# The first job's row maxima computed at the end of the token stage in front of each attention, in a two-layer decoder on one core

## The chip, the core and the metric

The program runs on one core of a Trainium2 chip. The metric is the device time of one execution in microseconds (us). The engines are TensorE (PE in the profile, its weight loads PEld), VectorE (DVE), ScalarE (ACT), GpSimd (POOL) and SyncE (SP), which here issues nearly all DMAs. All of them run their own instruction streams in order and meet at semaphores.

## The reference

Two decoder layers over x of 2 x 1024 tokens with 256 features (16 heads of 16), each layer post-normalised:

```
x = layernorm(x + L0_attn(x))          # ALiBi, heads 0-7 look back, heads 8-15 look forward
x = layernorm(x + L0_xattn(x, ctx))    # 154 context tokens, scores clipped at +-10000
x = layernorm(x + L0_ffn(x))           # 8 experts, top 2
x = layernorm(x + L1_attn(x))          # full attention
x = layernorm(x + L1_xattn(x, ctx))    # 154 context tokens
x = layernorm(x + L1_ffn(x))           # a causal attention (MLA), then 8 experts, top 2

attn = softmax(q @ k.T / 4)            # over the keys, for each head
out  = attn @ v
```

A softmax needs the maximum of each row of scores before the exponential.

## The kernel before

The program is a list of stages: t0, at0, t1, xa0, t2, routing, experts, t3, at1, t4, xa1, t5, mla, t6, routing, experts, t7. Between two stages every engine drains and adds to one semaphore, and waits for all five: a barrier. at0, at1 and mla are self-attentions, xa0 and xa1 cross-attentions, the t stages ("token stages") do projections, layer norms and the q, k, v matmuls. The five places at which a token stage is followed by an attention are t0/at0, t1/xa0, t3/at1, t4/xa1 and t5/mla.

**An attention stage.** The 16 heads are four sets of 4 heads and the batch has two entries, which makes 8 groups `(s, i)`: `s`, the slot, is 0 or 1 (first or second half of each tensor of queries and keys, 64 of 128 output rows; in at0 slot 0 looks back and slot 1 forward), `i` the rest. A group has two jobs, one for each half of the 1024 queries. A job first computes its row maxima: TensorE makes the scores of 128 queries against all keys that count ("A" events, `pe_max`, L1535 and the diagonal mask L1538; L1789 in the cross-attention) into one of two PSUM regions of two banks each (banks 0 to 3), and VectorE reduces them to one column (`dve_max`, L1651; L1637 where it also adds the mask; L1890 in the cross-attention). In the causal and ALiBi stages the first job has 6 such units and the second 16; in at1 every job has 16 of 1024 keys; in the cross-attentions every job has 4. Then the maxima are transposed ("MT", L1585, L1835), negated (L1658, L1898), split into three bf16 parts by four instructions on GpSimd (`pool_split`), and `load_max` (L1460, L1736) copies these by three DMAs on SP's queue into three extra rows of the queries. Only then can the job's scores with the maximum subtracted be made ("ST", `pe_scores`, L1559; L1807), exponentiated (L1618, L1874) and multiplied with v ("PV", L1577), copied out ("OC", L1678) and transposed and divided ("OT", L1592, L1691).

`plan()` simulates an attention stage with fixed costs and writes the order of all these events into `at.events`; TensorE and VectorE follow that list in order. `LEAD` is 8 us.

**The queue of SP in an attention stage** before: rows of ones for three groups, `load_group` of group 1 (three loads of queries, six of keys, in at0 two of ALiBi rows), `load_max` of job 0, in at0 `rows_and_weights` (weights of t1 and the whole x), then jobs and groups in turn. In the cross-attentions it is the queries of group 1 (three DMAs), then `load_max` of job 0.

**A token stage** has for each half of a batch entry (512 tokens, halves 0 to 3) one "unit" for each of two f (f = 0 and 1 are the two blocks of 128 outputs) of q and k, and two for v: two to eight matmuls each (L1074, L1077, L1088, L1082), in order half 0, half 1, half 2, half 3. A q or k unit is split into three bf16 parts (L981/L984 on ScalarE, L1188/L1185 on VectorE, L990 on ScalarE, L893 on GpSimd) and stored to DRAM by two DMAs (`store_unit`, L831; `q_halves`, `k_parts`). `make_plan()` lists all this as tasks with a cost and a lag, and `list_order` schedules them greedily by the length of the path behind each, tries 150 shifted ranks, and keeps the order with the earliest end. Tasks of one kind stay in order. Each engine follows its own list in order. The task `ahead` waits on SP until the stores of halves 0 and 1 have landed and loads group 0 of the attention (`load_first`; L679 and L683, or L667). t0 also holds the context's keys and values (`ContextPart`; its matmuls use banks 0 to 3), and at its end SP stores the values, two DMAs of 1 MB (`store_values`, L1300); the first OT of at0 waits for them on VectorE (`rows_free`).

`mstat2`, the tile of maxima, is cleared by VectorE as the first instruction of each attention stage (L1696, L1924), so that row shows when the stage begins.

## Time and profile before

| | us |
|---|---|
| runs shown (3) | 2197.24, 2198.05, 2199.29; median 2198.05 |
| the profiled execution's own time | 2198.73 |
| its span, first to last instruction | 2197.0 |
| PE busy | 1950.5 (89%) |
| DVE busy | 1282.9 (58%) |
| ACT busy | 1015.5 (46%) |
| POOL busy | 482.0 (22%) |

A busy share is a mean over 17 stages. The granted clock of TensorE has two levels, 1.2 and 2.4 GHz; a row of a window gives the mean of the two as a share of the full one (0.50 is 1.2 GHz throughout). Beside each instruction the timeline gives the idle time of the engine ahead of it and who ended it.

### The profile page before, as it was taken

How to read it: one execution, taken by the hardware profiler on the slowest of the kernel's cores; microseconds unless marked ns; L12 is line 12 of the kernel's file. 1: busy time of each engine (PE TensorE's matmuls, PEld its weight loads, DVE VectorE, ACT ScalarE, POOL GpSimd, SP SyncE). 2: the span in 40 equal slices, each digit the busy share in tenths (PEclk: the TensorE clock that was granted, in tenths of full speed). 3: DMA queues.
4: the chain of work that ended last, by engine and by line, in shares of the span. 5: the costliest groups of instructions: out<-in, count | busy, mean ns of one | idle time of the engine just before them, and what ended most of it. 6: DMA issues, size and time to landing. Idle time of an engine off the chain costs nothing. (4 is left out here: it accounts for less than half of the span.)

```text
span 2197.0 us, 32881 instructions
## 1 busy us (share of the span) xinstructions
PE 1950.5 (89%) x10990; PEld 1009.5 (46%) x10991; DVE 1282.9 (58%) x2302; ACT 1015.5 (46%) x1953; POOL 482.0 (22%) x825
## 2 busy tenths in 40 slices
PE   8799999787689999968999999987887999977993
PEld 4344445332656666633223222253453444464662
DVE  3578774686622222246888888646586787653114
ACT  3156665576211111133566666754542666632333
POOL 2221101323132222212100000022352101033441
PEclk9599999898689999988899999998997999977997
DMA  7643222420811000037221111034234333051224
GB/s 195 166 64 53 43 33 52 109 46 16 354 44 33 31 31 31 29 114 156 30 30 30 30 30 30 1 97 101 45 78 107 53 59 60 2 192 41 64 63 134
DMA packets 98871, 157.90 MB, mean 72 GB/s; under 512 B 31415, under 2 KB 78839, under 8 KB 93559
## 3 DMA queue, kind: packets, MB, share of 16 engines
q1 hardware_dynamic: 86898, 131.55, 26.0%
q0 software_dynamic: 7488, 20.46, 3.0%
q10 hardware_dynamic: 4352, 4.20, 0.6%
q8 instruction: 74, 1.21, 0.3%
q14 instruction: 59, 0.48, 0.1%
HBM read 110.44 MB, written 44.72 MB: 71 GB/s over the span
## 5 line engine op out<-in xcount | busy, mean ns | idle before, releaser
L1618 ACT ACTIVATE arena<-psum 128x512 f32<-128x512 f32 (+1 forms) x1120 | 574.8, 592 | 351.7 <-PE psum L1559 210.4
L1651 DVE TENSOR_REDUCE arena<-psum 128x1 f32<-128x1024 f32 (+3 forms) x352 | 400.4, 1172 | 87.0 <-PE psum L1535 62.8
L1535 PE MATMUL psum<-arena 96*128 96x512 bf16 (+7 forms) x1280 | 367.4, 371 | 24.7 <-DVE arena L1651 9.5
L1559 PE MATMUL psum<-arena 99*128 99x512 bf16 (+7 forms) x1280 | 365.9, 354 | 19.4 <-DMA arena<-arena 10.5
L1577 PE MATMUL psum<-arena 128*32 128x512 f32 (+3 forms) x2560 | 279.4, 538 | 0.7 <-ACT arena L1618 0.7
L1637 DVE CUSTOM_DVE_ANT_0 arena<-psum,arena 128x640 bf16<-128x640 f32 (+3 forms) x256 | 249.5, 1021 | 50.3 <-PE psum L1535 49.6
L2197 PE MATMUL psum<-arena 128*128 x780 | 270.3, 493 | 1.7 <-ACT arena L2251 1.2
L1535 PEld LDWEIGHTS psum<-arena 96*128 96x128 bf16 (+1 forms) x1280 | 100.7, 101 | 263.5 <-issue 88.4
L1559 PEld LDWEIGHTS psum<-arena 99*128 99x128 bf16 (+1 forms) x1280 | 124.5, 99 | 191.5 <-ACT arena L1618 83.3
L2301 DVE COPY arena<-psum 128x640 f32<-128x640 f32 (+1 forms) x78 | 59.3, 760 | 252.4 <-PE psum L2207 252.4
L2216 PE MATMUL psum<-arena 128*128 (+1 forms) x780 | 189.1, 384 | 2.1 <-DVE arena L2304 1.2
L2197 PEld LDWEIGHTS psum<-arena 128*128 128x128 f32 x780 | 143.5, 192 | 82.2 <-issue 24.5
L1666 POOL CAST arena<-arena 32x128 bf16<-32x128 f32 x48 | 13.6, 284 | 736.5 <-DVE arena L1658 736.5
L2216 PEld LDWEIGHTS psum<-arena 128*128 128x128 f32 (+1 forms) x780 | 138.3, 189 | 30.8 <-issue 16.0
L1074 PE MATMUL psum<-arena 128*128 128x512 f32 x240 | 116.2, 626 | 14.7 <-DMA arena<-in_xT 9.1
L2110 POOL DMA_INDIRECT arena<-x_rows,arena x78 | 76.1, 975 | 232.6 <-PE psum L2185 197.4
L2294 DVE TENSOR_TENSOR arena<-arena,psum 128x704 f32<-128x704 f32 x39 | 34.7, 891 | 155.1 <-PE psum L2197 155.1
L1890 DVE TENSOR_REDUCE arena<-psum 128x4 f32<-128x616 f32 x128 | 100.2, 796 | 36.2 <-PE psum L1789 35.5
L2146 POOL DMA_INDIRECT y_rows<-arena x78 | 77.2, 989 | 158.7 <-ACT arena L2268 158.4
L1874 ACT ACTIVATE arena<-psum 128x512 f32<-128x512 f32 x160 | 93.6, 604 | 38.7 <-PE psum L1807 37.4
L1577 PEld LDWEIGHTS psum<-arena 128*32 128x32 f32 x2560 | 60.9, 108 | 107.1 <-issue 67.2
L1562 PE MATMUL psum<-arena 128*128 128x128 bf16 x512 | 98.7, 221 | 0.0
(208 smaller groups left out, 2374.8 us busy)
## 6 DMA issues: line engine op xcount, KB each, us to landing
arena<-k_parts SPq DMA_DIRECT2D x144, 128.0 KB
q_halves<-arena SPq DMA_DIRECT2D x80, 192.0 KB, 3.0
arena<-q_halves SPq DMA_DIRECT2D x40, 384.0 KB, 4.7
arena<-in_L_ffn_up SPq DMA_DIRECT2D x8, 1408.0 KB, 17.4
arena<-q_halves SPq DMA_DIRECT2D x40, 256.0 KB, 5.2
k_parts<-arena SPq DMA_DIRECT2D x48, 192.0 KB, 3.2
arena<-in_L_ffn_down SPq DMA_DIRECT2D x9, 1024.0 KB, 13.0
arena<-y_rows SPq DMA_DIRECT2D x32, 256.0 KB, 4.2
```

Source lines behind the costliest of these rows:

```text
L1074: last = nc.tensor.matmul(ps[:, :], m, xt[:, c, :], start=(c == 0), stop=(c == DC - 1))
L1535: last = nc.tensor.matmul(dst[:, base + lo:base + hi], q[0:rows, qh, h, qb % 4 * P:qb % 4 * P + P], k[0:rows, h, key0 + lo:key0 + hi], sta ...
L1559: last = nc.tensor.matmul(b[:, at0:at0 + width], kk[0:rows, h, kb * P:kb * P + P], q[0:rows, qh, h, c0:c1], start=True, stop=diag is None)
L1562: last = nc.tensor.matmul(b[:, at0 + diag - c0:at0 + diag - c0 + P], identb, mask_right if at.modes[g] == "bwd" else mask_left, start=Fals ...
L1577: last = nc.tensor.matmul(bank[o_bank][32 * h:32 * h + 32, c0:c1], v_st[g % 2][:, kb, h, :], probs[k % at.ahead][:, h, c0:c1], start=first ...
L1618: nc.scalar.activation(probs[k % at.ahead][:, heads[0]:heads[-1] + 1, c0:c1], bank[st_bank[no % 3]][:, 0:len(heads) * width].rearrange("p ...
L1637: last = nc.vector.tensor_tensor_reduce(out=unread[:, turn % 2, n_h * width:n_h * width + width], in0=src[:, n_h * pitch:n_h * pitch + wid ...
L1651: nc.vector.tensor_reduce(dst, src, AX.X, ALU.max).then_inc(t("taken"), 1)
L1874: nc.scalar.activation(place(j, tile), src, ACT.Exp, scale=QSCALE).then_inc(t("p"), 1)
L1890: nc.vector.tensor_reduce(dst, src, AX.X, ALU.max).then_inc(t("taken"), 1)
L2197: last = nc.tensor.matmul(bank[2 * w + hf][:, 0:half], xT[:, s, c, :], wu[:, ds(e, 1), c, w, hf * half:hf * half + half].rearrange("p o f ...
L2216: last = nc.tensor.matmul(bank[7][:, 0:D], hT[0:fw[f], s, f, :], w2[f][0:fw[f], ds(e, 1), :].rearrange("p o d -> p (o d)"), start=(f == 0) ...
```

## The change

The code of the maxima moves into two classes, `SelfMaxima` and `CrossMaxima`, with the same instructions, so that the token stage in front can issue them too. The maxima of job 0 become tasks of that token stage: `eclear` (the clear, now on GpSimd), `early` and `etake` (the A units on TensorE and VectorE), `emove`, `eneg`, `esplit` and `eload` (the transpose, the negation, the split, and the load of the three parts). In at1 only 8 of the 16 units move, and the transpose and what follows stay in the attention stage. `early` waits for the loaded group and until banks 0 to 3 are no longer used by the token stage. The units of halves 0 and 1 are reordered so that those of f = 0, which make slot 0, come first; `ahead` waits for these stores alone, and in front of a cross-attention `ahead2` loads group 1 as well. The planner ranks `ahead`, `esplit` and `eload` and all in front of them first. The attention's plan starts with job 0's maxima landed. The stores of the context's values move behind `load_group` of group 1 in at0, and weights and x behind the loads of groups 1 and 2; the bias additions on GpSimd move to the end of the attention stage. ScalarE waits for the token stage's last stores at the third step of job 0 (at the fifth tile in a cross-attention).

```diff
-    if ("ahead", 0) in tail:
-        tail["ahead", 0] += 1000.0
+    for key in (("ahead", 0), ("esplit", 0), ("eload", 0)):
+        if key in tail:
+            tail[key] += 1000.0
...
-    return order, max(us for eng, us in free.items() if eng != "SP")
+    return order, max([us for eng, us in free.items() if eng != "SP"] + [end.get(("eload", 0), 0.0) - 2.0])
...
+        self.n_early = n_early or len(self.units[0])
+        self.moved_early = self.n_early == len(self.units[0])
...
+    def early_costs(self):
+        widths = [len(heads) * width for heads, qb, key0, width in self.units[0]]
+        masks = 0.0 if self.modes[0] == "full" else 0.06
+        return [(len(self.units[0][n][0]) * (masks + 0.07) + w / 1700, 0.1 + w * 1.06e-3) for n, w in enumerate(widths[0:self.n_early])]
...
+        self.early = [("A", 0, n) for n in range(self.n_early)] + ([("MT", 0)] if self.moved_early else [])
+        self.events, self.turn = [], {e: n for n, e in enumerate(self.early)}
...
+        n_mx, moved = self.n_early, int(self.moved_early)
+        taken, landed = [0.0] * len(self.early), {0: 1.0} if moved else {}
...
+                sp.dma_start(stk[0][1][at.mrow:at.mrow + 3, :, :], a["ones"][0:3]).then_inc(sem("att_ones0"), 16)
...
-            for half in range(n_halves):
-                for o in outs:
-                    if o[0] in ("latent", "logits"):
-                        units.append((o[0], o, None, half))
-                    elif o[0] in ("qk", "klat"):
-                        units += [(o[0], o, f, half) for f in range(2)]
-                    elif o[0] in ("v", "vlat"):
-                        units += [(o[0], o, None, p) for p in (2 * half, 2 * half + 1)]
-            per = len(units) // n_halves
+            for both in ((0, 1), (2, 3)):
+                these = []
+                for half in both:
+                    for o in outs:
+                        if o[0] in ("latent", "logits"):
+                            these.append((o[0], o, None, half, half))
+                        elif o[0] in ("qk", "klat"):
+                            these += [(o[0], o, f, half, half) for f in range(2)]
+                        elif o[0] in ("v", "vlat"):
+                            these += [(o[0], o, None, p, half) for p in (2 * half, 2 * half + 1)]
+                if following and both[0] == 0:
+                    first = [x for x in these if x[0] == "latent" or x[0] in ("qk", "klat") and x[2] == 0]
+                    these = first + [x for x in these if x not in first]
+                units += these
...
+            needed = [[u for u in qk_no if units[u][2] == f and units[u][4] < 2] for f in range(2)]
...
-                    task("SP", "ahead", 0, 5.0, 3.0, *[("store", v) for v in qk_no if v < half_end(1)])
+                    crossed = following.keys < S
+                    task("SP", "ahead", 0, 1.6 if crossed else 5.5, 3.5, *[("store", v) for v in needed[0]])
+                    if crossed:
+                        task("SP", "ahead2", 0, 1.6, 3.0, ("ahead", 0), ("tra", n_pairs - 1),
+                             *[("store", v) for v in needed[1]])
+                    free = ("att", n_pairs - 1), ("add", n_pairs - 1), ("cmove", 7), ("cbias", 3)
+                    task("POOL", "eclear", 0, 0.4, 0.2)
+                    for n, (us, us_dve) in enumerate(following.early_costs()):
+                        task("PE", "early", n, us, 0.2, ("ahead", 0), ("eclear", 0), ("etake", n - 2), *free)
+                        task("DVE", "etake", n, us_dve, 0.15, ("early", n))
+                    if following.moved_early:
+                        task("PE", "emove", 0, 0.3, 0.2, ("etake", n))
+                        task("DVE", "eneg", 0, 0.3, 0.15, ("emove", 0))
+                        task("POOL", "esplit", 0, 2.6 if crossed and following.clip else 2.0, 0.2, ("eneg", 0))
+                        task("SP", "eload", 0, 1.6, 2.0, ("esplit", 0))
...
-                        for place in range(NPLACE):
-                            wait(sp, out_sem(place), stored(nqk // 2))
+                        half_stored(sp, 0)
                         load_first(sp, following)
+                    elif kind == "ahead2":
+                        sp.wait_ge(t("tra_ps"), n_pairs)
+                        half_stored(sp, 1)
+                        load_queries(sp, following, 1)
+                    elif kind == "eload":
+                        following.maxima.load(sp, 0)
...
-                if context:
-                    context.store_values(sp)
...
+            def half_stored(sp, f):
+                for u in needed[f]:
+                    sp.wait_ge(out_sem(qk_no[u] % NPLACE), 32 * (qk_no[u] // NPLACE + 1))
+            def all_stored(eng):
+                for place in range(NPLACE if nqk else 0):
+                    eng.wait_ge(out_sem(place), stored(nqk))
+            if following:
+                following.places_free = all_stored
...
+            def banks_free(pe):
+                pe.wait_ge(sem("att_cleared"), 1)
+                if source == "proj":
+                    pe.wait_ge(t("att"), n_pairs)
+                    pe.wait_ge(t("r"), n_pairs)
+                if context:
+                    context.banks_free(pe)
...
+                    elif kind == "early":
+                        if n == 0:
+                            banks_free(pe)
+                        following.maxima.pe(pe, 0, n)
+                    elif kind == "emove":
+                        following.maxima.pe_move(pe, 0)
...
+                for n in (1, 2):
+                    sp.dma_start(stk[n][1][at.mrow:at.mrow + 3, :, :], a["ones"][0:3]).then_inc(t(f"ones{n}"), 16)
+                load_group(sp, at, 1)
+                if early_sp:
+                    early_sp(sp)
+                if not at.moved_early:
+                    maxima.load(sp, 0)
+                for g in range(ng):
+                    maxima.load(sp, 2 * g + 1)
+                    if g + 2 < ng:
+                        if g:
+                            sp.wait_ge(t("st_ps"), exps_before(at.job_start[2 * g]))
+                        load_group(sp, at, g + 2)
+                    if g + 1 < ng:
+                        maxima.load(sp, 2 * g + 2)
+                    if g == 0 and extra_sp:
+                        extra_sp(sp)
...
+                for j in range(int(at.moved_early), 4):
+                    maxima.pool_split(pool, j)
+                for g in range(2, ng):
+                    pool.wait_ge(t("pv"), last_step[2 * (g - 2) + 1] + 1)
+                    stage_values(g)
+                    for j in (2 * g, 2 * g + 1):
+                        maxima.pool_split(pool, j)
+                if bias:
+                    add_bias(pool, *bias, 1)
...
+                    if k == 2:
+                        at.places_free(act)
...
+                load_queries(sp, at, 2)
+                load_queries(sp, at, 3)
                 for g in range(ng):
-                    load_max(sp, 2 * g + 1)
-                    if g + 2 < ng:
-                        load_queries(sp, at, g + 2)
+                    maxima.load(sp, 2 * g + 1)
+                    if g + 4 < ng:
+                        load_queries(sp, at, g + 4)
                     if g + 1 < ng:
-                        load_max(sp, 2 * g + 2)
+                        maxima.load(sp, 2 * g + 2)
...
-        at1 = SelfAttention("at1", ("full", "full"), False, q_halves, k_scr)
+        at1 = SelfAttention("at1", ("full", "full"), False, q_halves, k_scr, 8)
...
-        self_attention_stage(at0, (2, W["t1"]["brow"]), rows_and_weights, context_part.values_stored)
+        self_attention_stage(at0, (2, W["t1"]["brow"]), context_part.store_values, rows_and_weights,
+                             context_part.values_stored)
```

## Rows read from the trace of the kernel before

**Rows 1.** The windows view: busy us (x instructions) by engine, granted clock, DMA share.

```profile
core 0: us, PE busy (x) PEld busy (x) DVE busy (x) ACT busy (x) POOL busy (x), PEclk, DMA share, GB/s
...
70.00:83.00 13.00, 10.85 (x40) 6.53 (x40) 5.38 (x20) 1.38 (x3) 1.45 (x2) 0.76 0.18 48
...
83.00:92.00 9.00, 7.59 (x35) 3.65 (x35) 6.85 (x8) 0.00 (x0) 3.48 (x7) 0.50 1.03 305
...
125.00:175.00 50.00, 49.43 (x382) 23.71 (x382) 38.96 (x72) 32.95 (x64) 4.75 (x13) 0.95 0.43 67
...
1666.00:1682.00 16.00, 12.42 (x49) 4.26 (x49) 13.25 (x23) 0.00 (x0) 4.85 (x11) 0.51 0.67 125
```

**Rows 2.** Timeline of TensorE, first self-attention: start, length, [idle before, releaser].

```profile
105.14 0.58 PE L1559 MATMUL psum<-arena 105*128 105x512 bf16 x1 [6.88 <-DMA arena<-arena]
...
125.03 0.61 PE L1559 MATMUL psum<-arena 105*128 105x512 bf16 x1 [0.56 <-DMA arena<-arena]
```

**Rows 3.** The clear of the maxima's tile, where each attention stage begins.

```profile
L1696 DVE MEMSET arena<- x3: 112/112/112, 82.9 to 1665.7; 128x64 f32 x3
...
401.33 0.11 DVE L1924 MEMSET arena<- 128x64 f32 x1 [4.70 <-SPq L2456]
```

**Rows 4.** Timeline of VectorE, first self-attention.

```profile
107.15 1.09 DVE L1637 CUSTOM_DVE_ANT_0 arena<-psum,arena 128x896 bf16<-128x896 f32 x1 [7.88 <-PE psum L1535]
...
118.26 1.21 DVE L1637 CUSTOM_DVE_ANT_0 arena<-psum,arena 128x1024 bf16<-128x1024 f32 x1
```

**Rows 5.** The page's groups by line: two reductions of the maxima.

```profile
L1651 DVE TENSOR_REDUCE arena<-psum 128x1 f32<-128x1024 f32 (+3 forms) x352 | 400.4, 1172 | 87.0 <-PE psum L1535 62.8 <-PE psum L1538 23.0
...
L1637 DVE CUSTOM_DVE_ANT_0 arena<-psum,arena 128x640 bf16<-128x640 f32 (+3 forms) x256 | 249.5, 1021 | 50.3 <-PE psum L1535 49.6
```

**Rows 6.** Timelines around the first cross-attention: TensorE, then GpSimd.

```profile
380.29 1.88 PE L1074 MATMUL psum<-arena 128*128 128x512 f32 x4
...
402.08 1.19 PE L1789 MATMUL psum<-arena 96*128 96x154 bf16 x8 [7.03 <-DMA arena<-q_halves]
...
414.08 1.49 PE L1807 MATMUL psum<-arena 99*128 99x512 bf16 x3
...
384.85 1.09 POOL L893 TENSOR_TENSOR arena<-arena 128x512 bf16<-128x512 f32 x1 [2.83 <-ACT arena L990]
```

**Rows 7.** Timelines around the full self-attention: TensorE, VectorE, ScalarE.

```profile
1041.22 2.17 PE L1535 MATMUL psum<-arena 96*128 96x512 bf16 x4 [0.19 <-DVE arena L1651]
...
1054.95 1.49 PE L1559 MATMUL psum<-arena 99*128 99x512 bf16 x3
...
1029.39 19.96 DVE L1651 TENSOR_REDUCE arena<-psum 128x1 f32<-128x1024 f32 x17 [0.81 <-PE psum L1535]
...
1017.63 0.69 ACT L981 ACTIVATE arena<-psum,arena 128x512 bf16<-128x512 f32 x1 [6.79 <-DMA q_halves<-arena]
```

**Rows 8.** Timeline of TensorE, causal self-attention.

```profile
1682.13 0.59 PE L1559 MATMUL psum<-arena 99*128 99x512 bf16 x1 [1.56 <-DMA arena<-arena]
...
1701.40 1.49 PE L1559 MATMUL psum<-arena 99*128 99x512 bf16 x3
```

**Rows 9.** SP's DMA issues: start, us of issuing, how many.

```profile
81.84 0.84 SPq L1300 DMA_DIRECT2D vx<-arena  x2
...
395.22 1.53 SPq L667 DMA_DIRECT2D arena<-q_halves  x3
...
409.05 8.23 SPq L1736 DMA_DIRECT2D arena<-arena  x6
...
1004.44 0.33 SPq L679 DMA_DIRECT2D arena<-q_halves  x1
```

**Rows 10.** Landing: loads of maxima; the page's row for the stores of queries.

```profile
L1460 SPq DMA_DIRECT2D arena<-arena x144: 502/589/1306, 94.1 to 1910.0; - x144
...
DMA to landing us min/median/max: 1.7/1.8/9.6
...
q_halves<-arena SPq DMA_DIRECT2D x80, 192.0 KB, 3.0
```

441 lines of the change are left out of this document (231 added, 210 removed).

## The prediction

> **What bounds the kernel now.** I read the windows view first. Inside a self-attention, once it runs, TensorE is the bound: busy 49.43 of 50 us in the window from 125 to 175, at a granted clock of 0.95, with VectorE at 38.96 [rows 1]. The start of a stage is another matter. From 83 to 92 and from 1666 to 1682 the clock is 0.50 and 0.51, the lower of the two levels, and ScalarE does nothing [rows 1]. The timelines say why. at0 begins at 82.9 [rows 3], but its first scores come at 105.14, after an idle time of 6.88 that a DMA ends: the load of the maxima [rows 2]. While TensorE waits there in order, the maxima of job 1 wait behind it, and VectorE idles 7.88 us [rows 4]. Job 1's scores start at 125.03, again released by that kind of load [rows 2], and only from there on is TensorE full. So the start is a chain of latencies: reductions, transpose, split, load. It stands five times in the program: first scores 22.2 us after the start of at0, 12.8 after that of xa0 (401.33 to 414.08), 16.4 after that of mla [rows 2, 3, 6, 8]; in at1 they come at 1054.95, 25.6 us after the first reduction at 1029.39 [rows 7].
>
> The token stages in front are not empty: TensorE is busy 10.85 of the last 13 us of t0 [rows 1]. What is moved there has to be paid wherever it finds no gap.
>
> **at0 and mla: what the move takes away.** The place that decides is the start of job 1's scores, since TensorE is full from there. Now it is 125.03 - 82.9 = 42.1 us after the start in at0, and 1701.40 - 1665.7 = 35.7 in mla [rows 2, 3, 8]. Afterwards the stage begins with job 1's 16 reductions, 1.021 us each: 16.3 us [rows 5]. I add 1.4 for job 0's copy-out and division (an estimate, from the mean of some 0.7 us that a 512-wide VectorE instruction has next to these rows) and 3 for waits on TensorE, between 0 and the 7.88 seen [rows 4]. From the last reduction (118.26 + 1.21) to job 1's scores at 125.03 it is 5.6 [rows 2, 4]. Sum: 26.3. at0 gains 42.1 - 26.3 = 15.8, mla 35.7 - 26.3 = 9.4. The bound below is the same with 7.9 for the waits, 4.9 less each; above, with none, 3 more.
>
> **What it puts into the stages in front.** In t0 the six units of the ALiBi job need the matmuls that now fill 83 to 92: 7.59 us busy at clock 0.50, so 3.8 at full clock [rows 1]. The two context stores of 0.84 leave t0's queue [rows 9]. Since TensorE has no gap to speak of, I take 3.5 us of growth, with 3.0 and 6.8 as ends. The split and load of the maxima (1.8 us on SP by 3 x 0.589 [rows 10]) I cost at nothing there: the planner ranks them first and the remaining v and k units cover them; without that cover they add up to the 5.6 above. In t5 TensorE waits more on norms, and the same matmuls cost between 0 and 3.8; I take 1.5.
>
> at0 has a new wait as well. The context's values are now stored behind group 1's load, and job 0's division on VectorE waits for them; all of job 1's reductions are queued behind it, and TensorE's next units behind those. Group 1 is eleven DMAs, so the stores go out some 9 us after the start. A DMA lands 1.7 us after its issue at best and 9.6 at worst [rows 10], and the division is due some 13 us after the start. The stall is 0 to 5; I take 2. The Trainium skill, DMA: Bandwidth & Descriptors, section "Queues, rings and completion order", says that each DMA engine consumes a queue's descriptors in ring order, so that the stores would wait for all of group 1; by that rule the stall would be the whole 5 and the time 2170.
>
> at0: 15.8 - 3.5 - 2 = 10.3. mla: 9.4 - 1.5 = 7.9.
>
> **at1.** Of the 17 reductions in 19.96 us [rows 7] eight move: 8 x 1.174 = 9.4 us, which is the whole chain's shortening, since transpose and split stay. Their 16 matmuls cost t3 2.17 per four at the low clock [rows 7], 8.7 in all, 4.3 at the full one. t3 had some gaps: ScalarE idled 6.79 us behind a store [rows 7]. But slot 0's units now need half 1's rows earlier. I take 4 (0 to 8.7), and 0.5 for the maxima's load, which comes 9.4 us sooner and closer behind group 1's. at1: 9.4 - 4 - 0.5 = 4.9.
>
> **xa0 and xa1.** The second unit's third part is done at 384.85 + 1.09 = 385.9 [rows 6]. Afterwards this unit is f = 0 of half 1, so `ahead` needs no more than it. Issuing and 3.0 of landing [rows 10] bring 390. From the load's issue to the first maxima it was 402.08 - 395.22 = 6.9: 397. From there to the maxima's load 409.05 - 402.08 = 7.0: 404 [rows 6, 9]. Three DMAs and their landing, 1.8 + 1.8, bring the first scores to 407.6, against 414.08: 6.5 us [rows 6, 10]. But this load is now in front of the barrier. SP issues it until 405.8, so the stage starts near 406.2 and no longer at 401.33, and job 1's maxima start about when they did before. Job 1's own scores then decide how much is kept, between 0 and 6.5. Loaded early, group 1 no longer holds job 2 up. I take 4, and the same for xa1, which lacks only the clip.
>
> The bias additions on GpSimd go to the stage's end, where GpSimd has little (4.75 of 50 us [rows 1]): nothing. The wait of ScalarE for the last stores costs nothing either: they land 3.0 us after issue [rows 10], about when the third step begins.
>
> **Sum.** 10.3 + 4 + 4.9 + 4 + 7.9 = 31.1. The profiled execution took 2198.73: 2167.6. The median shown is 0.7 below it, so 2167.
>
> **Rivals.**
>
> A: the token stages grow more than I allow, or job 1 keeps less; each term near its lower end: at0 15.8 - 6.8 - 5 = 4.0, at1 0.7, mla 5.6, the cross-attentions 0, together 10.3, so 2188. For it: TensorE is near full in t0 [rows 1], and the planner's costs are not the chip's. Against it: five independent terms.
>
> B: no change that can be told (0.2%, 4.4 us): what is gained at the start is lost to the barrier that comes as much later. For it: in xa0 the barrier moves by 4.9 of 6.5 us. Against it: the idle times of 6.88 and 7.88 in at0 are waits, not work. Time 2198.
>
> C: slower. The place is TensorE in the token stages: `early` waits in order for group 0, and all later units are queued behind it. In t3 the load began at 1004.44, and a store behind it freed ScalarE only at 1017.63 [rows 7, 9], so the group can take 13.2 us, where the plan has 9.0. TensorE would idle 4.2 us and then run at the low clock: a unit of 1.88 [rows 6] costs twice that, four of them 7.5 more. 11.7 in each of three stages and 1.8 in the two with the small load (6.9 against a plan of 5.1) are 38.7, against 31.1 gained: 2205. It decides from 31 us of such waits. Against it: in t1 the load lands about when the last unit ends, so nothing is behind it. The Trainium skill, TensorE: Matmul & The Clock Gate, section "HAM oscillation — how this bites in real kernels", warns that a wait for DMAs throttles the clock again each time; by that rule C's second half comes with its first, and the rows at 0.50 after TensorE's waits agree.
>
> D: all terms at their upper end: at0 15.8 - 3.0 + 3, mla 12.4, at1 9.4, 6.5 twice, 50.6 in all: 2147.
>
> **Chances.** My own case, a gain of 18 to 43 us (2155 to 2180), has 0.64, with 2167 as its time. A has 0.18, B 0.07, C 0.06, D 0.05. Below and above these I leave the rest out: the range of 2153 to 2188 takes in my own case and nearly all of A. A change of 0.2% (4.4 us) is about what a measurement of this kernel tells from none. Faster: 0.64 + 0.18 + 0.05, less 0.02 for A's tail, 0.85. Same 0.08, slower 0.07.
>
> **What would show it.** The profile afterwards should have reductions of job 0 inside t0, t1, t3, t4 and t5. Scores of job 0 should come within 3 us of the start of at0 and mla, and job 1's some 27 us after it. The starts of the stages, by the barrier, should be later relative to the token stage's own start by 3.5 in t0, 5 in t1, 4 in t3, 1.5 in t5. A wait of VectorE for the context's stores in at0 measures the 2 us. The prediction is wrong if the token stages' TensorE shows waits for group 0 longer than some 3 us each with units behind them, or if job 1's scores come no earlier than now.

## The result and the profile after

The changed kernel takes 2179.02 us (median of 4 runs, 2176.72 to 2181.22), the kernel before beside it 2198.67 (4 runs). The ratio is 0.9903, with a 95% interval of 0.9887 to 0.9919: faster by 1%, where the prediction had 2167 in a range of 2153 to 2188. The profiled execution took 2178.35 us, with a span of 2176.6, against 2198.73 and 2197.0: 20.4 less, where the prediction's sum had 31.1. One of the four runs of e6 below took 2214.57 us at a lower mean clock (0.894, the others 0.933 to 0.934) and is left out of its median.

Where the 20.4 us lie can be read from the first instruction behind each barrier. In the timeline of ScalarE or TensorE it is the one whose idle time is ended by a drain (L2456 before, L2580 after). Kernel before, ScalarE, starts of t1, t2, t4 and t5:

```profile
356.31 1.70 ACT L942 ACTIVATE arena<-arena 128x512 f32<-128x512 f32 x3 [3.82 <-DVEq L2456]
548.84 1.69 ACT L942 ACTIVATE arena<-arena 128x512 f32<-128x512 f32 x3 [1.55 <-SPq L2456]
1443.00 1.70 ACT L942 ACTIVATE arena<-arena 128x512 f32<-128x512 f32 x3 [3.43 <-DVEq L2456]
1590.54 1.70 ACT L942 ACTIVATE arena<-arena 128x512 f32<-128x512 f32 x3 [1.55 <-DVEq L2456]
```

Changed kernel, the same four, and below them TensorE's first instruction in at0, xa0 and mla:

```profile
345.02 1.70 ACT L1001 ACTIVATE arena<-arena 128x512 f32<-128x512 f32 x3 [3.81 <-DVEq L2580]
538.45 1.69 ACT L1001 ACTIVATE arena<-arena 128x512 f32<-128x512 f32 x3 [1.55 <-SPq L2580]
1424.36 1.70 ACT L1001 ACTIVATE arena<-arena 128x512 f32<-128x512 f32 x3 [3.43 <-DVEq L2580]
1573.72 1.69 ACT L1001 ACTIVATE arena<-arena 128x512 f32<-128x512 f32 x3 [1.55 <-DVEq L2580]
...
81.90 1.21 PE L1562 MATMUL psum<-arena 102*128 102x512 bf16 x4 [2.01 <-SPq L2580]
394.03 1.21 PE L1662 MATMUL psum<-arena 96*128 96x154 bf16 x8 [5.89 <-SPq L2580]
1650.28 1.25 PE L1562 MATMUL psum<-arena 96*128 96x512 bf16 x4 [2.72 <-SPq L2580]
```

A token stage and its attention are best taken as a pair, since the barrier between them has moved. From such rows, in us (t3 begins at 955.12 and 944.79, t6 at 1931.78 and 1912.11):

| pair | before | after | measured | predicted |
|---|---|---|---|---|
| t0 + at0 (to t1's start) | 356.31 | 345.02 | -11.3 | -10.3 |
| t1 + xa0 | 192.53 | 193.43 | +0.9 | -4 |
| t3 + at1 | 487.88 | 479.57 | -8.3 | -4.9 |
| t4 + xa1 | 147.54 | 149.36 | +1.8 | -4 |
| t5 + mla | 341.24 | 338.39 | -2.9 | -7.9 |

The other stages make up the last 0.7. So the sum is off by a third, and two pairs have the wrong sign.

**at0 and mla.** The stage starts as foretold: TensorE begins with job 1's maxima, and job 0's scores come 1.0 us after the start (before: 22.2 [rows 2, 3]). But job 1's scores come at 113.92, 32.0 after it, and not 26.3; in mla at 1680.84, 30.6 after it (before: 35.7 [rows 3, 8]). TensorE, then VectorE and GpSimd at the start of at0, then VectorE in mla:

```profile
82.90 0.64 PE L1805 MATMUL psum<-arena 105*128 105x512 bf16 x1
113.92 1.06 PE L1805 MATMUL psum<-arena 105*128 105x512 bf16 x2
1680.84 1.06 PE L1805 MATMUL psum<-arena 99*128 99x512 bf16 x2
...
86.56 0.83 DVE L1590 CUSTOM_DVE_ANT_0 arena<-psum,arena 128x640 bf16<-128x640 f32 x1 [5.88 <-POOL arena L1768]
103.19 0.43 DVE L1880 TENSOR_TENSOR arena<-psum,arena 128x256 f32<-128x256 f32 x1 [0.96 <-DMA vx<-arena]
85.00 0.84 POOL L1766 MEMSET arena<- 128x896 bf16 x1 [5.11 <-issue]
86.02 0.29 POOL L1768 COPY arena<-arena 128x128 bf16<-128x128 bf16 x1
1654.63 0.82 DVE L1590 CUSTOM_DVE_ANT_0 arena<-psum,arena 128x640 bf16<-128x640 f32 x1 [6.28 <-POOL arena L1768]
```

VectorE's first reduction waits for GpSimd. A reduction that adds its mask reads the mask from `wide_mask`, which GpSimd writes as its first work of the stage (`widen_masks`, L1766 to L1768), and GpSimd's first instruction comes 3.1 us after the barrier. In the kernel before, these 4.7 us lay behind job 0's reductions, which need no such mask, and show nowhere as a wait. The windows rows that answer to [rows 1]: TensorE's clock is 0.50 at the start of at0 as before, but mla's start now has 0.72 (before 0.51), and from 125 to 175 it is full.

```profile
core 0: us, PE busy (x) PEld busy (x) DVE busy (x) ACT busy (x) POOL busy (x), PEclk, DMA share, GB/s
82.00:91.00 9.00, 5.20 (x19) 2.25 (x19) 3.27 (x9) 2.33 (x4) 3.46 (x7) 0.50 0.70 144
125.00:175.00 50.00, 49.53 (x429) 25.24 (x432) 40.69 (x76) 33.24 (x67) 6.67 (x18) 1.00 0.45 100
1650.00:1666.00 16.00, 12.24 (x88) 5.91 (x88) 9.24 (x21) 5.63 (x11) 3.47 (x7) 0.72 0.71 132
```

**t0.** It ends 1.0 us earlier, although it took in six units. The kernel before lost time there that the prediction did not count. Its TensorE waited 1.98 us for VectorE, until 57.66, and from 60 to 75 it ran at the lower clock while busy all the time; in the changed kernel the same stretch is at the full one, and in e4, where t0 has the new order but no early units, too (TensorE's wait in the kernel before, then the window in the kernel before, the changed kernel and e4):

```profile
57.66 1.47 PE L1329 MATMUL psum<-arena 128*128 128x256 f32 x4 [1.98 <-DVE arena L1391]
...
60.00:75.00 15.00, 15.00 (x48) 7.39 (x47) 5.09 (x17) 2.47 (x5) 2.19 (x4) 0.50 0.48 124
60.00:75.00 15.00, 14.96 (x56) 8.29 (x55) 9.63 (x15) 6.04 (x10) 5.26 (x8) 1.00 0.43 107
60.00:75.00 15.00, 13.65 (x78) 7.67 (x76) 7.46 (x28) 1.84 (x4) 1.46 (x2) 1.00 0.23 57
```

At the full clock those 15 us of matmuls would take some 7.5 (an estimate from the two levels). All traces of kernels with the new order have 1.00 in this window. There is one trace of the kernel before; whether its other executions ran the same way is not known.

**The cross-attentions.** Around t1 and xa0, TensorE and then SP (start, us of issuing, how many DMAs):

```profile
380.50 0.69 PE L1662 MATMUL psum<-arena 96*128 96x154 bf16 x8 [3.01 <-DMA arena<-q_halves]
383.02 3.29 PE L1132 MATMUL psum<-arena 128*128 128x512 f32 x4
397.26 1.01 PE L1952 MATMUL psum<-arena 99*128 99x512 bf16 x2 [2.02 <-POOL arena L1930]
...
373.06 1.58 SPq L687 DMA_DIRECT2D arena<-q_halves  x3
389.05 1.85 SPq L1648 DMA_DIRECT2D arena<-arena  x3
390.95 2.61 SPq L873 DMA_DIRECT2D q_halves<-arena  x4
```

In t1 TensorE waits 3.01 us for group 0, whose load goes out at 373.06. Two units are queued behind the `early` matmuls; the first then takes 3.29 us instead of 1.88 [rows 6]. That is rival C's mechanism, 4.4 us of it, in the very stage for which the prediction excluded it. The last stores go out at 390.95, behind the maxima's load, and t1 ends 4 us later (345.02 to 394.03: 49.0, before 45.0). In xa0 the first scores wait 2.02 more for GpSimd's zero pads (L1930).

What decides is again when job 1's scores come, counted from the start of the token stage, since the barrier moved. In xa0, kernel before (start of t1 356.31) and changed kernel (345.02):

```profile
419.81 0.85 PE L1807 MATMUL psum<-arena 99*128 99x512 bf16 x2
408.64 0.61 PE L1952 MATMUL psum<-arena 99*128 99x512 bf16 x2 [1.78 <-DMA arena<-arena]
```

That is 63.5 us before and 63.6 after; from t4's start to job 1's scores in xa1 it is 61.9 (1504.92) and 63.4 (1487.78). Nothing was gained there, and nothing in the pairs.

**at1.** As foretold, with a better price: first scores 16.0 us after the start, job 1's 43.1 (before 52.3). t3 took 1.3 us more and not 4.

### The profile page after: what moved, and what is told of

It reads as the page before. It is cut to its first block and busy times, and to the rows that moved or that the text cites. A ratio compares the mean times of both kernels' runs of the same rounds, so it can differ in the third digit from the quotient of the medians.

```text
span 2176.6 us, 32928 instructions
## 1 busy us (share of the span) xinstructions
PE 1931.4 (89%) x10990; PEld 1002.7 (46%) x10991; DVE 1281.4 (59%) x2297; ACT 1014.9 (47%) x1953; POOL 483.0 (22%) x854
## 3 DMA queue, kind: packets, MB, share of 16 engines
q1 hardware_dynamic: 86898, 131.55, 26.4%
## 5 line engine op out<-in xcount | busy, mean ns | idle before, releaser
L1562 PE MATMUL psum<-arena 96*128 96x512 bf16 (+7 forms) x1280 | 362.6, 368 | 29.4 <-DVE arena L1590 11.6
L2014 ACT ACTIVATE arena<-psum 128x512 f32<-128x512 f32 x160 | 92.8, 602 | 33.4 <-PE psum L1952 31.7
```

Of the source, the lines that this page charges most:

```text
L1562: last = nc.tensor.matmul(dst[:, base + lo:base + hi], q[0:rows, qh, h, qb % 4 * P:qb % 4 * P + P], k[0:rows, h, key0 + lo:key0 + hi], sta ...
L2014: nc.scalar.activation(place(j, tile), src, ACT.Exp, scale=QSCALE).then_inc(t("p"), 1)
```

## The experiments

Every time stands beside the kernel before, run on the same chip; stage lengths are from one profiled execution each. Stages whose program is the same differ between executions: the pair t1 and xa0 by up to 4 us in the same code, t5 by 2, xa0 alone by 1.8 (142.4, 142.6 and 144.2 in e7, e1 and e5), and t0, which waits for the first inputs, ended at 77.9 to 83.0 in the twelve traces with early maxima in it and is left out of comparisons. Effects below that are not read from lengths but from the wait itself.

### e1: GpSimd's first work made in the token stage

```diff
                     elif kind == "eclear":
                         nc.gpsimd.memset(mstat2, 0.0).then_inc(sem("att_cleared"), 1)
+                        if following.keys == S and following.modes[0] != "full":
+                            widen_masks(following)
+                        if following.keys < S:
+                            clear_pads()
```

> The changed kernel, with GpSimd's first work of the attention stages (the wide masks of at0 and mla, the zero pads behind the keys of xa0 and xa1) made in the token stage in front. Theory 1, job 1 is held by GpSimd: in at0 VectorE's first reduction waits until 86.56, 4.8 us after the start at 81.8, for the masks; in mla until 1654.63, 4.4 after; in xa0 and xa1 the first scores wait 2.0 for the pads and TensorE's units of job 1 stand behind them. Then at0 and mla become some 4 us shorter each, job 1's scores coming 28 and 26 us after the start and no longer 32.1 and 30.6, and xa0 and xa1 up to 2 each: some 12 us in all, 2167. Rival 2, job 1's start is set by the latencies and the low clock of TensorE: the 16 reductions wait as much elsewhere, and the gain is below 3 us in all, 2176 or more; t0 and t5 may grow by the 1.4 us that GpSimd spends.

Measured: 2172.37 us, ratio 0.9876 (0.9826 to 0.9927). mla became 257.8 us long (261.8), job 1's scores came after 27.4. xa0 and xa1 lost their wait of 2.0, but TensorE then waited 3.05 and 3.54 us for the maxima of job 1 (1.78 and 1.72 in the changed kernel), and the pairs became only 0.2 and 1.0 shorter. Of the 12 us expected some 6 came, by the two ratios. And at0 stayed at 262.9 (263.1), and job 1's scores at 32.4. VectorE there:

```profile
78.52 0.82 DVE L1607 CUSTOM_DVE_ANT_0 arena<-psum,arena 128x640 bf16<-128x640 f32 x1 [1.81 <-PE psum L1579]
99.56 0.43 DVE L1888 TENSOR_TENSOR arena<-psum,arena 128x256 f32<-128x256 f32 x1 [6.01 <-DMA vx<-arena]
```

It starts 0.6 us after the stage (at 77.93), and then waits 6.01 us for the stores of the context's values instead of 0.96. They land 21.6 us after the start, as in the changed kernel (103.19 - 81.90 = 21.3): theory 1 holds for mla, gives almost nothing in the cross-attentions, and falls for at0, where a second wait lay under the first.

### e2: the semaphores cleared behind GpSimd's first work

```diff
-                        for other, handle in sems.items():
-                            if kind and other.startswith(kind):
-                                eng.sem_clear(handle)
+                        clear_names[0] = clear_names_of
+                        if not progs.get("clears"):
+                            clear_names_of()
...
                 stage_values(0)
                 stage_values(1)
+                clear_names[0]()
...
+                clear_names[0]()
                 for j in range(1, len(at.jobs)):
                     maxima.pool_split(pool, j)
```

> The changed kernel, with GpSimd's clearing of the token stage's semaphores moved in each attention stage from in front of its first work to behind it. Theory 1a: the 2.8 to 3.2 us between a stage's start and GpSimd's first instruction (85.00 in at0, 1653.06 in mla, 396.81 in xa0) are the clearing of semaphores, which the page does not count as busy. Then the masks are ready some 1.8 us after the start, at0 and mla become 3 us shorter, xa0 and xa1 2: 10 in all, 2169. Rival 1b: the time is a fixed latency of GpSimd at a stage's start: its first instruction comes as late as now, and the time stays at 2179. Rival 2 as in the run with GpSimd's work moved: below 3 us.

Measured: 2176.22 us, ratio 0.9893 (0.9842 to 0.9943). GpSimd in at0, where TensorE's first matmul stands at 78.22 too:

```profile
78.22 0.85 POOL L1767 MEMSET arena<- 128x896 bf16 x1 [2.03 <-SPq L2588]
```

Its first instruction follows the barrier at once, and so it does in the other four attentions: theory 1a holds, the 3 us are the clearing. mla 259.4, job 1's scores after 28.5; at0 again unmoved (263.1), VectorE waiting 5.71 for the stores. t1 was 51.6, 2.6 more than in the changed kernel with the same program, and xa0 147.7, 3.3 more, though its first scores came 2.2 earlier; TensorE's clock over 99 us in the middle of it was 0.91, against 0.95 in the changed kernel and in e1. So the 10 us expected did not come; why xa0 was slow was not separated.

### e5 and e6: the stores of the values back in t0

```diff
                     elif kind == "eload":
                         following.maxima.load(sp, 0)
+                        if context:
+                            context.store_values(sp)
```

e5 is e1 with this, e6 the changed kernel with this alone.

> The kernel of e1_pool_first (GpSimd's masks and pads made in the token stage), and the two stores of the context's values issued in t0 again, behind the maxima's load. Theory 6, two waits of VectorE lie over one another in at0: the masks (until 4.8 us after the start) and the context's values, whose stores land 21.4 to 21.6 us after the start in both kernels, so that taking the first away only made the second grow from 0.96 to 6.01. With both gone job 1's scores come some 26.5 us after the start of at0 instead of 32.4, and at0 is 5 to 6 shorter: 257 to 258 us. The price in t0 is up to 1 us of SP. Rival 7: at0 is full of work on TensorE later on, so an earlier job 1 gives nothing and at0 stays at 263; or the 2 MB of the stores now hold up the stores of the last units or group 1, and t0 or at0's job 2 gets later by as much.

> The changed kernel with only the two stores of the context's values issued in t0, the masks still made at the start of at0. Theory 6: VectorE still starts 4.8 us after the stage, so only the wait of 0.96 us goes: at0 is 1 us shorter, 262. With e1_pool_first (masks alone, at0 262.9) and e5 (both) it fills the table of the two waits: neither 263.1, masks alone 262.9, stores alone 262, both 257 to 258. Rival 7 expects all four within 1 us of one another.

Measured: e5 2172.43 us, ratio 0.9864 (0.9843 to 0.9884); e6 2179.74, 0.9908 (0.9878 to 0.9938). What decides is at0's length, and when job 1's scores come after its start:

| | masks in at0 | masks in t0 |
|---|---|---|
| values' stores in at0 | 263.1, 32.0 (changed kernel) | 262.9, 32.4 (e1) |
| values' stores in t0 | 261.8, 31.7 (e6) | 257.6, 26.4 (e5) |

e5, VectorE and TensorE; the stage starts at 81.91:

```profile
97.22 0.43 DVE L1890 TENSOR_TENSOR arena<-psum,arena 128x256 f32<-128x256 f32 x1
108.34 1.49 PE L1815 MATMUL psum<-arena 105*128 105x512 bf16 x3
```

The division runs without a wait, and job 1's scores come 26.4 us after the start, the prediction's 26.3 (26.0 to 27.9 in the six later kernels, which have both moved too). Theory 6 holds: each wait alone is worth 0.2 to 1.3 us, both together 5.5. The stores' own time is in the DMA view (KB each, median us to landing), in the changed kernel, in the kernel before and in e5:

```profile
vx<-arena SPq DMA_DIRECT2D x2, 1024.0 KB, 11.5
vx<-arena SPq DMA_DIRECT2D x2, 1024.0 KB, 5.9
vx<-arena SPq DMA_DIRECT2D x2, 1024.0 KB, 5.1
```

The same two stores land in half the time when they go out in t0. Issued behind group 1's eleven loads they take 11.5 (e1: 12.2): it is what stood in front of them, and not their size alone, that made them late.

### e3 and e4: what the early maxima are worth

```diff
-        self.early = [("A", 0, n) for n in range(4)] + [("MT", 0)]
+        self.early = []
...
-        self.n_early = n_early or len(self.units[0])
+        self.n_early = 0
```

The first of these, in the cross-attentions, is e3; e4 has both.

> The changed kernel, with the first maxima of the two cross-attentions made inside those stages again; the order of the units and the early loads of groups 0 and 1 stay. Theory 3: in the cross-attentions the early maxima give nothing, because the token stage in front ends as much later as the attention starts earlier: TensorE waits 3.01 us for group 0 in t1 and 1.27 in t4 with units queued behind, and the splitting on GpSimd and the maxima's load on SP stand in front of the last stores. Then t1 and t4 shrink by 4 to 4.6, xa0 and xa1 grow by some 3 each, and the time is 2176 or a little less. Rival 4: the growth of t1 and t4 comes from the new order of the units and from the two loads in SP's queue, so it stays, and the lost maxima cost 3 us each: 2185.

> The changed kernel with no early maxima at all: what is left is the order of the units (first slot first), the early loads of group 0 (and 1 in the cross-attentions), the context's value stores and the bias additions at their new places. Theory 1 and 3: the whole gain is the early maxima's, so at0, at1 and mla come back to 273, 415 and 266 us, within 1 us each, and the time is that of the kernel before within 3 us, 2198. Rival 4: the order of the units lengthens t1 and t4 by 4 each: 2206. Rival 5: the moved stores and bias additions gave part of the gain (t0 became 1.0 shorter although it took in six units' matmuls and reductions): 2193 or less.

Measured: e3 2180.75 us, ratio 0.9916 (0.9889 to 0.9943); e4 2194.66, 0.9968 (0.9947 to 0.999). Against the kernel before beside them (2200.64) that is 19.9 less and 6.0 less, so the early maxima of the three self-attentions are 13.9 of e3's 19.9. The 6.0 (2.2 to 11.7 by the interval) that stay without any early maxima are more than the 3 expected and what rival 5 says: part of the gain is not the maxima's. e4's t0 ends at 75.9, 7.0 earlier than in the kernel before, whose low clock there is shown above. at0 came back to the 273 expected and t1 and t4 to 44.7 and 44.8; at1, at 413.6, lies 1.4 under what was expected, and mla, at 269.2, lies 3.2 over it, which stays open. In e3 t1 and t4 fell to 45.3 and 45.4 as theory 3 says, so the order of the units costs nothing there (rival 4 is out), but xa0 and xa1 grew by 5.8 and 4.1 and not by 3: the pairs are 195.5 and 149.9, 2.1 and 0.5 above the changed kernel, so the early maxima did not cost in the cross-attentions; what they gave lies within the differences of the same code, and the whole time (2176 expected) doesn't tell the two kernels apart. And both lie above the kernel before, 192.5 and 147.5, with the same maxima at the same place; e4 has 195.2 and 150.7. TensorE in e3's xa0, which starts at 390.23:

```profile
405.33 1.46 PE L1952 MATMUL psum<-arena 99*128 99x512 bf16 x3 [4.88 <-DMA arena<-arena]
```

and the landing times of all loads of maxima in e3's cross-attentions, from the view of their line:

```profile
DMA to landing us min/median/max: 1.7/1.8/8.3
```

TensorE waits 4.88 us for the maxima's load (e4: 4.59; none in the kernel before), and one such load takes 8.3 us instead of 1.8. The change put the queries of groups 2 and 3 ahead of the first maxima's load in SP's queue, where it had been one group. e8 and e9 take that up.

### e7: all 16 maxima of at1 in t3

```diff
-        at1 = SelfAttention("at1", ("full", "full"), False, q_halves, k_scr, 8)
+        at1 = SelfAttention("at1", ("full", "full"), False, q_halves, k_scr, 16)
```

> The kernel of e5, and in the full attention all 16 first maxima made in t3, with transpose, split and load. Theory 8, each of those reductions that stands at at1's start costs its 1.17 us there and little in t3, where VectorE and TensorE have gaps (t3 took 1.3 us more for the first eight): first scores of at1 16.0 earlier, job 1's scores from 41.9 to 43.3 down to some 26 to 30, at1 shorter by 8 to 12, t3 longer by 2 to 5: a further gain of 5 to 8. Rival 9: t3's gaps are used up by the first eight, the next eight come at their full price of 9.4 in t3 and the sum stays as it is or gets worse.

Measured: 2166.16 us, ratio 0.984 (0.9824 to 0.9857). at1 fell from 403.7 to 392.1 us, t3 rose from 73.7 to 86.1: 478.2 for the pair, 477.5 in e5. Rival 9 holds: the first eight cost t3 1.3 us for 9.6 gained, the next eight 12.4 for 11.6. The 6 us by which this kernel was faster than e5 do not lie in what was changed: of 7.6 between the two profiled executions 3.9 lie in t1 and xa0, whose program is the same (191.6 against 195.6), and there job 1's scores came 62.6 us after t1's start against 66.2.

### e8 and e9: the cross-attention's early maxima behind the last unit

```diff
-                    free = ("att", n_pairs - 1), ("add", n_pairs - 1), ("cmove", 7), ("cbias", 3)
+                    free = ("unit", len(units) - 1 if crossed else -1), ("att", n_pairs - 1), ("add", n_pairs - 1), ("cmove", 7), ("cbias", 3)
...
-                        task("POOL", "esplit", 0, 2.6 if crossed and following.clip else 2.0, 0.2, ("eneg", 0))
-                        task("SP", "eload", 0, 1.6, 2.0, ("esplit", 0))
+                        if not crossed:
+                            task("POOL", "esplit", 0, 2.0, 0.2, ("eneg", 0))
+                            task("SP", "eload", 0, 1.6, 2.0, ("esplit", 0))
...
+                maxima.load(sp, 0)
                 load_queries(sp, at, 2)
                 load_queries(sp, at, 3)
...
+                maxima.pool_split(pool, 0)
+                clear_names[0]()
                 for j in range(1, len(at.jobs)):
                     maxima.pool_split(pool, j)
```

Both are e5 with this; GpSimd's clearing is moved in all attentions, as in e2, and the plan of a cross-attention takes job 0's maxima as landed at 6.0. e9 then has another queue for SP in the cross-attentions:

```diff
-                maxima.load(sp, 0)
-                load_queries(sp, at, 2)
-                load_queries(sp, at, 3)
...
+                behind = {1: 2, 2: 3, 3: 4, 5: 5, 7: 6, 9: 7}
+                for j in range(len(at.jobs)):
+                    maxima.load(sp, j)
+                    if j in behind:
+                        load_queries(sp, at, behind[j])
```

> The kernel of e5, and in the token stages before the cross-attentions (t1, t4) the early maxima's matmuls behind the last unit, with the reductions, the transpose and the copy still in the token stage, but the split and the load as the first work of GpSimd and SP in the cross-attention, where GpSimd clears its semaphores only behind the split. Theory 3a: what t1 and t4 lost was TensorE waiting for group 0 with units behind it, and the split and load in front of the last stores; they come back to some 45.4 us as in e3_self_only, while the first scores come 6.5 us after the start and job 1's some 12 to 13: t1 and xa0 together 188 to 190 (before 192.5, changed 193.4, e3 195.5), t4 and xa1 together 145 to 147 (147.5, 149.3, 149.9). Rival 10: job 2 and the later ones are held by VectorE and the later loads anyway, so that xa0 and xa1 give back what t1 and t4 gain, and the sums stay at 193 and 149.

> The kernel of e8, with SP's order in the cross-attentions changed: the loads of the first and second job's maxima go out before groups 2 and 3, which follow one at a time. Theory 11, in e8 the load of job 1's maxima was issued at 391.60 behind the six DMAs of groups 2 and 3 (388.45 to 391.56) and landed only at 401.1, 7.7 us after its own issue, where it lands some 1.2 us after it with nothing in front: the small load waits in the queue behind the large ones. With the order changed job 1's scores come some 12 us after the start of xa0 (17.5 in e8, 14.7 in the changed kernel) and 13 in xa1 (18.7 and 14.5), and t1 and xa0 together take 190 to 192 us (e5 195.5, e8 198.1), t4 and xa1 145 to 147 (148.7, 149.5). Rival 10: the later jobs are bound by VectorE and by the distance between a job's maxima and its scores, and the sums stay at 195 and 149.

Measured: e8 2174.02 us, ratio 0.9876 (0.9858 to 0.9893), pairs 198.1 and 149.6, where 188 to 190 and 145 to 147 were expected: a miss. e9 2156.91, 0.9797 (0.9775 to 0.982), pairs 186.2 and 142.7. In e8 t1 and t4 fell to 46.0 and 45.2 as expected, and the first scores came 5.9 after xa0's start, but job 1's after 17.5. SP and TensorE of e8 in xa0 (start 383.70):

```profile
388.45 3.11 SPq L688 DMA_DIRECT2D arena<-q_halves  x6
391.60 1.77 SPq L1669 DMA_DIRECT2D arena<-arena  x3
...
401.18 1.03 PE L1966 MATMUL psum<-arena 99*128 99x512 bf16 x2 [5.42 <-DMA arena<-arena]
```

and its loads of maxima in the cross-attentions:

```profile
DMA to landing us min/median/max: 1.7/1.7/8.6
```

The load of 3 x 4 KB was issued at 391.60 behind six loads of up to 384 KB, and its scores start 9.6 us later, TensorE idle for 5.42 of them. e9, with the two loads of maxima in front (start 384.96):

```profile
388.13 5.57 SPq L1669 DMA_DIRECT2D arena<-arena  x6
393.74 1.52 SPq L688 DMA_DIRECT2D arena<-q_halves  x3
```

```profile
DMA to landing us min/median/max: 1.7/1.7/3.4
```

No load of maxima takes over 3.4 us now, job 1's scores come after 12.0 and 11.5, which is 57.8 and 56.8 us after the start of the token stage (before 63.5 and 61.9), and the pairs are 6.4 and 4.9 us below the kernel before, more than theory 11 expected. It holds. The Trainium skill, DMA: Bandwidth & Descriptors, section "Queues, rings and completion order", says that each DMA engine consumes a queue's descriptors in ring order; by that rule, the 8.6 and the 3.4 agree. Of e8's distance to e9 in xa0, 11.7 us, 5.4 stand at job 1's start; the rest builds up over the later jobs and was not separated. TensorE's clock may have a share in it: from 396 to 415 it was 0.73 in e8 and 1.00 in e9.

### e10, e11, e12: the bias additions of xa0

VectorE and GpSimd near the end of xa0 in the changed kernel, and VectorE in the kernel before:

```profile
514.44 7.78 DVE L2027 SCALAR_TENSOR_TENSOR arena<-arena 128x512 f32<-128x512 f32 x1 [2.89 <-ACT arena L2014]
512.14 9.53 POOL L1491 TENSOR_TENSOR arena<-arena 128x256 f32<-128x256 f32 x16
```

```profile
527.48 7.04 DVE L1906 SCALAR_TENSOR_TENSOR arena<-arena 128x512 f32<-128x512 f32 x1 [3.28 <-ACT arena L1874]
```

A clip whose median is 0.68 us takes 7.78: it ends at 522.22, half a microsecond behind the last of GpSimd's 16 additions (521.67). TensorE idles 6.63 us behind it (5.90 in the kernel before).

```diff
                 for j in range(1, len(at.jobs)):
                     maxima.pool_split(pool, j)
-                if bias:
+                    if at.clip and j <= 12:
+                        add_bias(pool, *bias, 1, j + 3, j + 4)
+                if bias and not at.clip:
                     add_bias(pool, *bias, 1)
```

The first four (in e12 eight) additions stand in e10 ahead of job 1's split, in e11 and e12 behind it.

> The kernel of e5, with the 16 bias additions of xa0 no longer in one piece behind the last split but four at its start and one behind each of twelve splits. Theory 12: at the end of xa0 VectorE's clip takes 7.78 us instead of 0.69 (7.04 in the kernel before), until GpSimd is through its 16 additions (512.14 to 521.67): GpSimd holds VectorE off while it adds without a pause. Spread out, no clip takes over 1.5 us, and xa0 becomes 6 to 8 us shorter, 136 to 138 instead of 144. Rival 13: every addition costs VectorE its 0.6 us wherever it stands, and VectorE is what bounds xa0, so 9 us are lost in small pieces and xa0 stays within 2 us of 144.

> The kernel of e9 with the bias additions of xa0 spread: four behind job 1's split, then one behind each of the next twelve. Theory 12 with what e10 showed (xa0 3.1 us shorter, no clip over 1.6 us): xa0 some 3 us shorter than in e9, 137 to 138, and the time 2154. Rival 13: with the earlier jobs of e9 VectorE has less room, every addition costs its 0.6 us, and xa0 stays at 140.

> The same with eight additions behind job 1's split, where VectorE waits for maxima and scores, and one behind each of the next eight. If the additions cost nothing where VectorE is waiting (theory 12), four more there save up to 2.4 us over the kernel with four: xa0 135 to 137, the time 2152 to 2154. If they hold up job 2's split, which comes some 8 us behind job 1's, by their 4.9 us (rival 14), xa0 is 1 to 2 us longer than with four.

Measured: e10 2169.25 us, ratio 0.9858 (0.9836 to 0.9879), on e5; e11 2153.89, 0.978 (0.9762 to 0.9798), and e12 2154.24, 0.9789 (0.9771 to 0.9806), both on e9. The view of e10's line of clips (min, median, max ns):

```profile
L2039 DVE SCALAR_TENSOR_TENSOR arena<-arena x80: 670/684/1521, 393.0 to 526.7; 128x512 f32<-128x512 f32 x80
```

No clip takes over 1.6 us in e10, and xa0 is 3.1, 2.0 and 2.2 us shorter than in the kernel each builds on. The first stands against the longest of three xa0 with the same program, so it may be as little as 1.3; and the whole times of e11, e12 and e9 agree within their intervals. Theory 12 has the mechanism, and at most half the size it gave for e10. Four or eight at the start makes no difference. In these runs TensorE's clock in the middle of xa0 was 0.91 and 0.93, against 0.96 and 0.97 in e9 and e5, so part of the gain may be hidden; that was not separated. The Trainium skill, SBUF — State Buffer, section "SBUF: two separate sides", says that VectorE, in an instruction with two operands in SBUF, and GpSimd share a pair of ports under an exclusive lock. The clip is such an instruction; the rule explains why it waits, and not why it waits for all sixteen.

## Why the prediction was right and where it was wrong

The direction and the range were right, and so was the place: the start of job 1's scores decides in a self-attention. The time lies at the far end of the prediction's own case (2155 to 2180), 12 us above its 2167, and it lies there with the help of luck, since several terms were wrong in opposite directions. Step by step:

- **at0, 15.8.** Measured 10.1 for job 1's start. The 26.3 us were worked out rightly (26.4 in e5, 26.0 to 27.9 later). What was missing is the wide masks: `widen_masks` was among the stage's first work all along, 4.7 us from the barrier, and the page before shows it nowhere as a wait. The argument took away the cover, job 0's reductions, and did not ask who else had been under it.
- **The stall for the context's stores, 2 (0 to 5).** Measured 0.96, right only because the masks had made VectorE late. Without them it is 6.01, above the range's end. The landing was put at some 9 us after the start plus up to 9.6; the stores went out after 8.2 and landed after 21.3. The same stores need 5.1 to 5.9 us with group 1's loads not in front of them and 11.5 to 12.2 with them, so the prediction's second reading, by which they wait for all of group 1 and the stall is the whole 5, was the better one.
- **t0, 3.5.** t0 came out 1.0 shorter. The base was wrong: the kernel before spent 15 us of t0 at the lower clock, which [rows 1] show in part (0.76 from 70 to 83), and the changed kernel did not. Against e4, which has the new order without the six units and ends t0 at 75.9, the twelve traces with them are 2.0 to 7.1 later, so the units may well cost what was forecast; e4 has one trace, so this isn't shown. With at0's 10.3 the pair makes 11.3 against 10.3: the gain in at0, put too high by 3.5 (15.8 - 2 against 10.3), and the growth of t0, put too high by 4.5, cancel. That is luck.
- **mla, 7.9.** The step that failed is again "job 1's start", 30.6 and not 26.3; 3.1 of these 4.3 go with the masks (e1: 27.4 and a stage 4.0 shorter). So its start came 5.1 us earlier and the stage became 4.2 shorter, where 9.4 was forecast. t5's 1.5 was right (1.4).
- **at1, 4.9.** 9.6 in at1 as worked out (8.9). The 4 for t3 was mis-sized: 1.3. With eight more the gaps are gone and each costs what it saves (e7).
- **The cross-attentions, "I take 4, and the same for xa1".** This is the term that failed most: +0.9 and +1.8 instead of -8, which is 10.7 us, as much as the whole sum was off; the errors of the other pairs cancel. The prediction let job 1's scores decide what is kept, "between 0 and 6.5", and that is what happened, at the lower end: counted from the token stage's start they came 0.1 and 1.5 us later than before. The runs show three things in the way. TensorE waited for group 0 in t1 with two units behind it, while the prediction let the load land behind the last unit: `ahead` went out 28.0 us after t1's start, not 33.7. The pads of GpSimd held the first scores for 2.0, though with them gone the next wait grew and the pairs gained only 0.2 and 1.0 (e1). And "loaded early, group 1 no longer holds job 2 up" was paid for by two groups in front of the first small load; this is the one that e9 turned into a gain of 6.4 and 4.9 (e3, e8, e9). The new order of the units was rightly costed at nothing (e3).
- **Rival B**, the barrier gives back what is gained, is what happened in these two pairs. **Rival C** was real in t1, at 4.4 us; in t4 the wait was 1.27, in the other three token stages there was none. The prediction's own sign of being wrong, waits for group 0 over some 3 us each with units behind them, was thus just met in one of five stages (3.01).
- **The bias additions, "nothing"** holds for the change, but in xa0 their place had held up one clip by 6.4 us before as well, which the reading missed. Spreading them gave back 3.1 us at most.

Put right by these runs, the kernel of e11 takes 2153.89 us, 2.2% less than the kernel before and more than twice the change's gain. What stays open is what the six units cost t0 by themselves, why mla was longer in e4, and what sets TensorE's clock in xa0, 0.91 to 0.97.

## What to carry to other kernels

When work is taken from the front of a stage, list everything that was hidden under it, on every engine and queue, before counting the gain: waits that end under a longer one show nowhere in the profile, and two of them may have to go together before either pays. Work that another engine does first in a stage belongs into the stage in front as well. And a small load that a chain waits for goes out ahead of large ones, even if that makes the large ones late.

## What the runs showed of the hardware

- GpSimd's first instruction came 2.8 to 3.1 us after the barrier in front of an attention. It was clearing semaphores one by one, which the page calls "issue" and counts nowhere as busy. With the clearing behind the first work that instruction came at once (e2: at 78.22, together with TensorE's), and at0 and mla were no longer for it (263.1 and 259.4, against 263.1 and 261.8).
- A VectorE instruction on two SBUF operands of 0.68 us took 7.0, 7.8 and 9.8 us (kernel before, changed kernel, e5) while GpSimd ran 16 additions of 0.6 us back to back, and not over 1.6 us when they were apart (e10).
- A load of 4 KB landed 1.7 us after its issue alone, and up to 8.6 us behind six loads of up to 384 KB (e8). Two stores of 1 MB took 5.1 to 5.9 us to land when they went out in t0, and 11.5 to 12.2 right behind eleven loads.
- TensorE stayed at the lower clock from 59 to 75 in the kernel before, after a wait of 1.98 us, while the profile shows it busy 15.00 of the 15 us from 60 on; in the changed kernel a wait of 3.01 was followed by a unit of 3.29 us instead of 1.88.
